# Pairs of experts' odd pieces in shared tiles: 73 tiles in place of 80 in a mixture-of-experts tower

## The reference

```python
probs = softmax(xt @ router_w.T + router_b)          # 16 experts
topk_p, topk_i = lax.top_k(probs, 2)                 # every row goes to two
gates = jnp.sum(onehot(topk_i) * topk_p[..., None], axis=1)
def expert_step(acc, (w1e, b1e, w2e, b2e, ge)):      # w1e 512x128, w2e 128x512
    h = gelu(xt @ w1e.T + b1e)
    y = h @ w2e.T + b2e
    return acc + y * ge[:, None]
```

## Time and profile before

| | us |
|---|---|
| median of 3 runs (671.29 to 671.98) | 671.81 |
| the profiled execution | 673.02 |
| its span, first to last instruction | 671.2 |
| TensorE busy | 615.3 (92%) |
| VectorE busy | 569.6 (85%) |
| ScalarE busy | 496.4 (74%) |
| GpSimd busy | 424.3 (63%) |
| mean granted clock of TensorE | 0.982 |

### The profile page before, as it was taken

One profiled execution on the slowest core, in us unless ns is written; L12 is line 12 of the kernel. 1 busy time (PEld: TensorE's weight loads), 2 busy tenths in 40 slices (PEclk: granted clock), 3 DMA queues, 4 the chain that ended last, 5 costly groups with the idle time before them and its releaser, 6 DMA issues.

```text
span 671.2 us, 24622 instructions
## 1 busy us (share of the span) xinstructions
PE 615.3 (92%) x7952; PEld 580.8 (87%) x7952; DVE 569.6 (85%) x1800; ACT 496.4 (74%) x1258; POOL 424.3 (63%) x446
## 2 busy tenths in 40 slices
PE   3899999999999999999998877999999999999970
PEld 3799999999999999999997866789988989888760
DVE  3888888888988888988899878997887887989896
ACT  3678888666776777676555457778888888999884
POOL 0244444488787786667666677777777666666571
PEclk9999999999999999999999979999999999999995
DMA  8988887778988888878876114445543435555665
GB/s 320 379 277 284 282 276 272 244 260 274 284 272 287 275 277 280 252 233 261 261 252 194 57 56 100 111 127 168 169 142 116 119 114 157 159 175 161 188 225 201
DMA packets 76063, 143.29 MB, mean 213 GB/s; under 512 B 14110, under 2 KB 59817, under 8 KB 68005
## 3 DMA queue, kind: packets, MB, share of 16 engines
q1 hardware_dynamic: 66080, 122.96, 58.6%
q0 software_dynamic: 9280, 17.21, 7.3%
q10 hardware_dynamic: 580, 1.55, 0.6%
HBM read 117.96 MB, written 25.66 MB: 214 GB/s over the span
## 4 chain that ended last, share of the span: by engine, by line
PE 54%; DVE 10%; issue 7%; DMA 5%; POOL 3%; ACT 1%; SPq 0%; POOLq 0%; DVEq 0%; ACTq 0%
PE pair L1298 19%; PE pair L1458 11%; PE pair L1476 10%; DMA patches<-sent 4%; PE pair L1344 3%; PE pair L1308 3%; PE pair L1432 2%; DVE patches L1114 2%; POOL sent L1250 1%; POOL back L1274 1%; PE pair L1313 1%; PE pair L1404 1%; PE pair L1373 1%; DMA field<-back 1%; PE pair L1323 1%
## 5 line engine op out<-in xcount | busy, mean ns | idle before, releaser
L1274 POOL DMA_INDIRECT back<-patches x160 | 156.7, 979 | 68.3 <-issue 53.9
L1250 POOL DMA_INDIRECT sent<-pay,slot_own x130 | 155.5, 1196 | 40.4 <-issue 38.2
L1298 PE MATMUL pair<-field,patches 128*128 128x128 f32 x1280 | 158.4, 280 | 9.0 <-DMA patches<-in_x 9.0
L1298 PEld LDWEIGHTS pair<-field,patches 128*128 128x128 f32 x1280 | 149.5, 194 | 9.0 <-issue 9.0
L685 ACT ACTIVATE pair<-pair,b1s 128x256 f32<-128x256 f32 x320 | 123.7, 448 | 28.4 <-PE pair L1458 26.5
L610 ACT ACTIVATE gate<-pair,lbias 128x128 f32<-128x128 f32 x260 | 74.3, 368 | 88.3 <-PE pair L1313 88.3
L1458 PE MATMUL pair<-patches,ex_hi 128*128 128x256 f16 x640 | 110.9, 275 | 5.4 <-DVE patches L1114 3.9
L1476 PE MATMUL pair<-ex_hi,patches 128*128 x1280 | 111.4, 219 | 2.9 <-DVE patches L1114 1.5
L1262 POOL TENSOR_TENSOR rstd<-veps,cst 128x2 f32<-128x2 f32 (+1 forms) x68 | 57.4, 845 | 84.5 <-DVE veps L813 84.1
L1298 PE MATMUL pair<-field 128*128 128x128 f16 x1664 | 103.4, 219 | 2.1 <-DVE field L856 2.1
L1298 PEld LDWEIGHTS pair<-field 128*128 128x128 f16 x1664 | 99.1, 98 | 3.1 <-issue 1.3
(11 more groups left out here) (152 smaller groups left out, 1232.6 us busy)
## 6 DMA issues: line engine op xcount, KB each, us to landing
patches<-in_x SPq DMA_DIRECT2D x62, 1152.0 KB
patches<-sent SPq DMA_DIRECT2D x80, 130.0 KB
field<-in_we SPq DMA_DIRECT2D x64, 128.0 KB
field<-back SPq DMA_DIRECT2D x10, 768.0 KB
patches<-in_b SPq DMA_DIRECT2D x80, 64.0 KB
field<-in_pos SPq DMA_DIRECT2D x65, 64.0 KB
out_tower<-h SPq DMA_DIRECT2D x10, 384.0 KB
patches<-in_x SPq DMA_DIRECT2D x128, 24.0 KB
```

Source lines behind the costliest of these rows:

```text
L1250: pool.indirect_dma_start(sent, bass.IndirectOffsetOnAxis(ap=slot_own[:, g % 4, choice, col:col + 1], axis=0), pay[:, t % NP, :], None, bo ...
L1274: pool.indirect_dma_start(back, bass.IndirectOffsetOnAxis(ap=dsti[j % NO][:, k:k + 1], axis=0), yo[j % NO][:, k, :], None, bounds_check=2 ...
L1298: last = pe.matmul(bank_of, l, w_, start=(c == 0), stop=(c == KC and k == 1))
```

## The change

The number of tiles goes from 80 to 73. Each expert's rows are now counted in pieces of 128: `HALVES_ALL` = 145 of them in the worst case, and TILES_B is half of that, rounded up. An expert's even number of pieces makes tiles of 256 rows as before. Its odd last piece, if there is one, goes into half of one of eight **dual** tiles (tiles 32, 35, ... 53), which hold the pieces of two experts.

- The late plan gets a fourth section of 16 entries (the odd pieces) and one for what lies between; it looks up 33 + 16 = 49 entries in place of 48. Its last three lines work from PSUM directly, in both plans, and the early plan's piece 8 and part of its piece 7 are gone, with the late plan computing what they did.
- A dual tile's rows come in two loads of 128 rows. Its second half's expert is copied by DMA from `ex_hi` and `ex_lo` to one of two fixed buffers, `at_hand`, which with a two-row bias buffer `b2_two` lies where `pay` was.
- TensorE does a dual tile's up matmuls as 24 of 128 columns, ScalarE its gelus as eight of 128x128, VectorE its destinations as two.
- Chunks: eight of 6 tokens, of which four begin in slots 60, 64, 68 and 72 and four are loaded in slots 74 to 77; then 17 tokens in four pieces (`LAST`, 5 + 4 + 4 + 4) after all scatters, into the memory of `ex_hi`.

```diff
-TILES_B = (2 * TOKENS - E) // ROWS + E
+HALVES_ALL = (2 * TOKENS - E) // P + E
+TILES_B = -(-HALVES_ALL // HALVES)
+DUALS = E // 2
+DUAL = tuple(range(EARLY, EARLY + 3 * DUALS, 3))
+PAIRS = TILES_B - EARLY - DUALS
+LOOKUPS = PAIRS + 2 * DUALS
-FIRST_SPAN, SECOND_SPAN = 32, 54
+FIRST_SPAN, SECOND_SPAN, GATED = 32, 48, 54
+CHUNKS = [(t, CHUNK) for t in range(0, SECOND_SPAN, CHUNK)]
+LAST = [(48, 5), (53, 4), (57, 4), (61, 4)]
-FIRST_IN = EARLY + E
-SECOND_IN = (2 * P * SECOND_SPAN - E) // ROWS + E
-BACK_AT = (52, 57, 62, 67, 71, 74)
+FIRST_IN = EARLY + E + DUALS
+SECOND_IN = (2 * P * SECOND_SPAN - E) // ROWS + E + DUALS
+BACK_AT = (60, 64, 68, 72)
...
-        LOADS = {**{at: m for m, at in enumerate(BACK_AT)}, 76: 6, 78: 7, 80: 8}
+        LOADS = {**{at: m for m, at in enumerate(BACK_AT)}, 74: 4, 75: 5, 76: 6, 77: 7}
... SyncE
+                    if j in DUAL:
+                        for half in range(HALVES):
+                            sp.reg_load(at_half, tabi[0:1, 1, k + half:k + half + 1])
+                            row = sp.snap(at_half, min_val=0, max_val=E * CAP)
+                            sp.dma_start(xt[j % 4][:, half, :], sent[bass.ds(row, P), :]).then_inc(xt_in[j % 4], 16)
+                j = n + 2
+                if j in DUAL:
+                    d = DUAL.index(j)
+                    if d >= 2:
+                        through(sp, down_ps, DUAL[d - 2])
+                        through(sp, y_done, DUAL[d - 2])
+                    k = column(j)
+                    sp.reg_load(at_other, tabi[0:1, 0, k + 1:k + 2])
+                    e = sp.snap(at_other, min_val=0, max_val=E - 1)
+                    for part_of, whole_of in enumerate((ex_hi, ex_lo)):
+                        sp.dma_start(at_hand[d % 2][:, part_of, :, :],
+                                     whole_of[:, bass.ds(e, 1), :, :].rearrange("p a m f -> p (a m) f")
+                                     ).then_inc(hand_in[d % 2], 16)
+                    sp.dma_start(b2_two[d % 2][:, 1, :],
+                                 b2[bass.ds(e, 1), :].rearrange("a h -> (a h)").partition_broadcast(P)
+                                 ).then_inc(b2_two_in[d % 2], 16)
...
             tiles_landed(sp, TILES_B)
-            for m in range(BETWEEN + AHEAD_OF_END, len(CHUNKS)):
-                load_back(m)
+            for k, (t, size) in enumerate(LAST):
+                sp.dma_start(last_rows[k], back.rearrange("(b r) h -> b r h", r=2 * T)[:, 2 * t:2 * (t + size), :]
+                             ).then_inc(last_in[k], 16)
             for m in range(BETWEEN, len(CHUNKS)):
                 store_out(m)
... ScalarE
+                width = ROWS // len(experts)
                 for i in range(2):
+                    for a, e in enumerate(experts):
+                        cols = slice(i * ROWS + a * width, i * ROWS + (a + 1) * width)
+                        last = act.activation(up[:, cols], up[:, cols], ACT.Gelu,
+                                              bias=b1s[:, bass.ds(e * FC + 2 * half + i, 1)], scale=1.0 / E_SCALE)
... VectorE, the late plan's first piece
+                        tiles_of(full, late, P - 1, cst[:, C_EBASE:C_TOK])
+                        by(late, dve.tensor_tensor(ceiled[:, :, :], ceiled[:, :, :],
+                                                   full.unsqueeze(1).to_broadcast([P, 2, E]), ALU.min))
+                        by(late, dve.tensor_tensor(odd_base, full, cst[:, C_EBASE:C_TOK], ALU.add))
+                        seen(late)
+                        by(late, dve.tensor_tensor(over[:, 0:E], count[:, :], odd_base, ALU.is_gt))
+                        by(late, dve.tensor_tensor(base[1], ceiled[:, 0, :], took[1], ALU.add))
+                        by(late, dve.tensor_tensor(lengths[:, 0:E], ceiled[:, 0, :], took[0], ALU.subtract))
+                        by(late, dve.tensor_tensor(lengths[:, 2 * E:3 * E], full, ceiled[:, 1, :], ALU.subtract))
+                        by(late, dve.tensor_tensor(base[2], ceiled[:, 1, :], cst[:, C_EBASE:C_TOK], ALU.add))
+                        seen(late)
... TensorE
+            def up_of_two(n, half, i, e):
+                d, c = DUAL.index(n), 2 * half + i
+                x_hi, x_lo = xTs[n % 2][:, 0:ROWS], xTs[n % 2][:, ROWS:2 * ROWS]
+                for a in range(HALVES):
+                    if a == 1 and half == 0 and i == 0:
+                        pe.wait_ge(hand_in[d % 2], (d // 2 + 1) * 32)
+                    rows = slice(a * P, (a + 1) * P)
+                    for k, (part_of, r) in enumerate(((0, x_hi), (0, x_lo), (1, x_hi))):
+                        if a == 0:
+                            w1 = (ex_hi, ex_lo)[part_of][:, bass.ds(e, 1), 0, c * P:(c + 1) * P].rearrange(
+                                "p a f -> p (a f)")
+                        else:
+                            w1 = at_hand[d % 2][:, part_of, 0, c * P:(c + 1) * P]
+                        last = pe.matmul(ps_up(n, half)[:, i * ROWS + a * P:i * ROWS + (a + 1) * P], w1, r[:, rows],
+                                         start=(k == 0), stop=(k == 2))
...
-                        for k, (h_, w_) in enumerate(((hhi, ex_hi), (hlo, ex_hi), (hhi, ex_lo))):
+                        for k, (h_, part_of) in enumerate(((hhi, 0), (hlo, 0), (hhi, 1))):
                             for a in range(HALVES):
+                                if a == 1 and j in DUAL:
+                                    w2 = at_hand[DUAL.index(j) % 2][:, part_of, 1, c * HID:(c + 1) * HID]
```

More of the change, by code:

```diff
@@ L305, in tower @@
         b2_in = [sem(f"b2_in{i}") for i in range(4)]
+        hand_in = [sem(f"hand_in{i}") for i in range(2)]
+        b2_two_in = [sem(f"b2_two_in{i}") for i in range(2)]
         in_ps, in_hi, in_done = sem("in_ps"), sem("in_hi"), sem("in_done")
@@ L315, in tower @@
         out_done = sem("out_done")
+        last_in = [sem(f"last_in{i}") for i in range(len(LAST))]
+        last_first, last_scaled, last_done = sem("last_first"), sem("last_scaled"), sem("last_done")
         N_FIRST, N_WEIGHTS, N_CONST = 2, 4, 3
@@ L323, in slots @@
         def slots(step, tile, steps_first=False):
-            for n in range(-5, AHEAD + TILES_B + 4):
+            for n in range(-5, AHEAD + max(TILES_B + 4, BACK_AT[-1] + 10)):
                 if n <= AHEAD or steps_first:
@@ L418, in tiles_landed @@
         def tiles_landed(eng, tiles):
-            for q in range(NO):
-                eng.wait_ge(y_out[q], 16 * HALVES * len(range(q, tiles, NO)))
+            for j in range(tiles - NO, tiles):
+                eng.wait_ge(y_out[j % NO], (j // NO + 1) * 16 * HALVES)
         def norms(n):
@@ L446, in _ @@
             at_row, at_expert, at_pad = (sp.alloc_register(name) for name in ("at_row", "at_expert", "at_pad"))
+            at_half, at_other = (sp.alloc_register(name) for name in ("at_half", "at_other"))
             def load_patches(t):
@@ L867, in step @@
                     dve.tensor_copy(padi[:, :], count[0:1, :]).then_inc(pad_rows, 1)
-                for span, g in enumerate((3, 6)):
+                for span, g in enumerate((3, 5)):
                     if n == ready(g) + 1:
@@ L1074, in plan_piece @@
                     seen(late)
+                    by(late, dve.tensor_scalar(expert, expert, odd_half, None, ALU.add))
+                    seen(late)
                 if k == 5:
@@ L1455, in step_b @@
                             c = 2 * half + i
+                            if n in DUAL:
+                                last = up_of_two(n, half, i, e)
+                                continue
                             for k, (w_, r) in enumerate(((ex_hi, x_hi), (ex_hi, x_lo), (ex_lo, x_hi))):
```

270 lines of the change are left out of this document (173 added, 97 removed).

## The result

The changed kernel took 665.64 us in the median of five runs (664.47 to 668.86), the kernel before 671.56 beside it on the same chip. The ratio is 0.9922, 95% interval 0.9900 to 0.9944: faster by 5.2 us by the ratio, 5.9 by the medians. The forecast was 659.5, a gain of 12.3. So the sign is right and the time lies just inside the range (up to 666.0), but less than half of the gain arrived.

A forecast was written before the change was run, and what follows sets the result against it. TensorE was taken to bound the main tile stretch at 2.952 us per tile. Terms -20.7 + 1.0 + 2.9 - 0.5 - 1.7 + 6.7 = -12.3 from 671.8 gave 659.5 us, range 655.5 to 666.

The forecast's parts named there:

- Seven tiles fewer: In the TensorE-bound stretch or the one behind it, seven tiles removed at 2.952 us each: -20.7 us.
- The early plan: Five operations of pieces 7 and 8 and one of piece 6 go, three move to slot 55: -0.5 us.
- The late plan: Operations added between tiles where VectorE has no idle time, so nothing hides them: +2.9 us, ends +1.5 and +3.9.
- The dual tiles on TensorE, ScalarE and VectorE: In eight dual tiles, narrow matmuls cost the same, and extra gelu and destination work fits in idle time: 0 us.
- The copies: SyncE's weight copies for dual tiles land just before TensorE wants them, with thin margin: +1.0 us, ends 0 to +6.
- The back phase: Loads of 768 KB from `back` delay gathered rows in three places instead of five: -1.7 us, ends -2.5 and 0.
- The tail: From the last bias addition (Y) to the end, Y + 26.3 against Y + 19.6: +6.7 us, ends +4.5 and +9.5.
- VectorE's path: In the tail, VectorE's remaining chunks, gates and 17 tokens, then 2.6 us to the end: Y + 25.4.
- the queue's path: In the tail, 8.5 MB to move, loads at 336 and stores at 390 GB/s, plus 2 us for scatters: Y + 26.
- Copies hold TensorE up: Rival: slow copies inside SBUF make TensorE wait before each dual tile's fourth up matmul; 679 us at 90 GB/s, chance 0.06.
- The long tail: Rival: the tail has more gathers than the queue can move, 8.5 MB at 285 GB/s: +11.2, 664.0 us, chance 0.15.
- the short one: Rival: VectorE's tail path of Y + 25.4 or less holds and copies cost nothing: tail +5, 656.1 us, chance 0.18.

The follow-up runs named there:

- the last experiment: The changed kernel with the late plan's pieces in every second slot, both dual-tile bias rows on ScalarE's queue and chunk 4 loaded earlier: 660.45 us, ratio 0.9820.
- the four traces: First trace of the changed kernel, the same kernel run again (665.82 us), and two later kernels with the same code up to the end of the duals.
- the kernel with the three edits together: The changed kernel with the second bias row on ScalarE's queue, GpSimd adding in chunks 6 and 7, and chunk 4 loaded earlier: 662.39 us, ratio 0.9874.

## Why the prediction was right or wrong

*Seven tiles fewer, -20.7: right.* Outside the changed places the period is unchanged, (501.50 - 457.27)/15 = 2.949 us.

*The early plan, -0.5: not contradicted.* Instance 0 came at 402.38 against 403.61; over all these traces at 402.0 to 403.6, 402.9 on average, so -0.7. The scatter is larger than that, so the traces don't tell -0.5 from nothing.

*The late plan, +2.9: right.* Instances 7 and 13 in VectorE's order of time, with the wait that ends the stretch:

```profile
427.88 1.21 DVE L1231 TENSOR_TENSOR patches<-pair,patches 128x1024 f16<-128x1024 f32 x1
...
450.12 0.42 DVE L1239 CAST patches<-pair 128x256 f16<-128x256 f32 x1 [0.97 <-PE pair L1585]
...
451.12 1.21 DVE L1231 TENSOR_TENSOR patches<-pair,patches 128x1024 f16<-128x1024 f32 x1
```

(451.12 - 427.88)/6 = 3.87 us per tile, where 3.9 was forecast against 3.41, and +3.0 for the stretch. "Nothing hides it" was right for the slots as they stood; the last experiment shows that the free slots beside them could.

*The dual tiles on TensorE, ScalarE and VectorE, nothing: right.* The stretch without copies runs at 53.12 for 18 tiles. The eight narrow gelus, forecast at 2.2 us, in ScalarE's order of time:

```profile
504.73 2.15 ACT L768 ACTIVATE pair<-pair,b1s 128x128 f32<-128x128 f32 x8 [0.49 <-PE pair L1569]
```

*The copies, +1.0: wrong, +5.0 in this trace and +4.2 on average, within the ends of 0 and +6.* This is the step that failed. The prediction asked whether the copies would land before TensorE wants them, 5.3 us after the first one's issue. In one of the four traces they always did, in another with one wait of 0.3; in the others TensorE waited for `ex_lo`, up to 0.72 and 0.99 us. In the changed kernel run again it landed 5.05 us after the first copy's issue (526.85 to 531.90), which is inside the 5.3, but the copies had left late, and TensorE wanted them 4.4 us after that issue.

The prediction wrote "SyncE is not late for others: its slot has 2.95 us and about 1.4 us more of issues; the bias of tile j-1 is wanted three slots on". The issues cost more: from 507.09, the end of the rows' issue, to 510.15, the end of the extra bias, 3.06 us, since the first copy's issue took 1.32 and the pause for the register load ahead of it 0.46. And the bias of tile j-1 isn't all that matters: behind it stand the rows of the next tile, in the same queue. They left at 511.73, 2.0 late against the pace of 2.95, and TensorE waited 0.52. Not counted either were the two loads of half a tile with a register load each, and that the three slots together hold ten issues. The prediction listed them in part, priced them as time for the copies, and didn't follow the queue on to the next tile.

What the experiments settle is that the copies make this whole cost. How it divides is rougher: about two thirds stay with a quarter of the bytes, and the long register loads of TensorE come and go with the bytes. Part of the cost shows as no wait at all: in 36 to 54 TensorE is busy 53.9 to 54.3 us in the four traces and 53.11 without copies, with the same matmuls, and why wasn't traced. What makes it differ by 2 us from trace to trace is open; single issues of 1.3 to 2 us, such as at 507.55, fall at other places in each, and without slack they would show, but that was only argued; the trace with a quarter of the bytes has four of 1.0 to 1.3 us in 36 to 54 as well.

Another small wait, about 0.2 us before the up matmuls, is put down to "issue". It falls on the matmul whose address depends on a register, and in the stretch 503 to 575 of this trace there are five of these, 1.1 us in all; in the kernel before there is none. Three of the five stand behind a wait for rows, the two others (548.60 and 567.60) behind a register load of 0.56 and 0.57 us. Where the kernel before waited for rows, from 577 us on, it has four of them as well, 0.9 us. In the kernel with one bias row on ScalarE there are five in 36 to 54 without any wait for a transfer.

*The back phase, -1.7: better, -3.3.* 54 to the last instance takes 54.10 = 18 x 2.951 + 1.0, where before it was 78.04 = 25 x 2.951 + 4.3. Of the loads that were thought to delay rows, at 0.8 each, one does so, by 0.3 us in TensorE's waits of this stretch.

*The tail, +6.7: right in kind, +8.2 in this trace.* VectorE in order of time, from the last bias addition to its last operation:

```profile
634.56 0.42 DVE L1246 SCALAR_TENSOR_TENSOR patches<-pair,patches 128x256 f32<-128x256 f32 x1 [0.33 <-PE pair L1635]
...
641.94 1.66 DVE L1312 SCALAR_TENSOR_TENSOR h<-field,gates,h 128x128 f32<-128x128 f32 x6 [0.78 <-DMA field<-back]
643.90 0.96 DVE L1323 TENSOR_TENSOR h<-h,field 128x768 f32<-128x768 f32 x1 [0.30 <-ACT field L755]
...
651.13 0.34 DVE L1298 TENSOR_REDUCE total<-lg 128x11 f32<-128x176 f32 x1 [0.74 <-ACT top L748]
...
659.10 0.69 DVE L1345 TENSOR_TENSOR h<-h,ex_hi 128x512 f32<-128x512 f32 x1
```

VectorE's path had been put at Y + 25.4 with 2.6 us after its last addition, so at Y + 22.8 for that addition. It ended at 659.79, Y + 25.2. The difference is its waits: 0.78 for chunk 4, and 1.6 for ScalarE (0.30 at 643.90 and at 649.43, 0.74 for the exponents, 0.27 at 653.64), which the sum had left out. Then 2.6 us to the end, as forecast. SyncE and the chain show the rest:

```profile
630.94 0.35 SPq L566 DMA_DIRECT2D out_tower<-h  x1
631.34 6.88 SPq L560 DMA_DIRECT2D field<-back  x3
```

```profile
638.73 8.71 DMA field<-back
```

Chunk 4's load stands behind the store of chunk 1, and chunk 7's, issued at 638.73, took 8.71 us, where the load that the kernel before issued at 658.79 took 4.63. The queue is full from 641 to 659 (share 1.01). Both paths of the forecast are there and near each other: relieving VectorE of two additions moved the end by nothing, and loading chunk 4 early moved VectorE's end by 1.1 us and the end by about half of that, or by nothing that one trace can tell. Which of the two is later in the last 3 us isn't settled; the last store's landing came 2.4 to 4.0 us after VectorE's end in these traces.

Beside the tail the prediction had set the Trainium skill (SBUF — State Buffer, "Summary: rules for kernel authors") with about 358 GB/s between HBM and SBUF. This tail moved 378 over 18 us and 400 in a stretch of 5 (645 to 650 us), loads and stores together by the view's count. The measurement is above the page, and it decides; the 378 lies between the 336 and the 390 that the queue's path took for loads and for stores. The prediction's remark that the fastest stretch of the trace before, 319 GB/s, stays below the page's figure was a misreading: that is the fastest of the tail, and the token phase of the same trace has this window.

```profile
16.00:33.00 17.00, 13.61 (x182) 12.76 (x183) 13.76 (x44) 9.99 (x28) 3.95 (x6) 1.00 1.04 380
```

That the queue would be no bound, as the page's rate had it, isn't borne out: it is full for 18 of the 27.8 us, with 27.84 x 322 = 8.96 MB to move, where 8.5 were counted.

*The rivals.* "Copies hold TensorE up" named the right cause and a part of the place: in the four traces no copy was near the 1.7 us late that would have cost the whole gain, and some waits are for the rows behind the copies. The long tail (+11.2) and the short one (+5) lie on both sides of +8.2. In sum, by the trace against the forecast: copies +4.0, tail +1.5, back phase -1.6, early plan -0.7, the rest +0.3, so 3.5 worse than -12.3. The other 2.9 between -8.8 and the medians' -5.9 lie in how each profiled execution stood to its median. The traces show two places that vary in the changed kernel, the dual stretch (2.1 us) and the tail; whether they explain all of it stays open.

## What to carry to other kernels

When a transfer is added to a queue-issuing engine, ask first for the next thing in its program order and how much slack that has, and sum the issues with their register loads over as many slots as the work repeats in; the new transfer's own time counts from when the queue comes to issue it. Its bytes can cost something apart from any wait for it, here in another engine's register loads. Work that an engine has to do between tiles costs less if it is cut so that free slots lie between the pieces. Before merging tensors to save a DMA, look at the addresses that other engines build from them.

## What the runs showed of the hardware

- An issue with a register-held address takes SyncE 0.33 to 0.54 us and about 0.45 more for its register load; single ones took 1.3 to 2.0 us (1.32 at 507.55, 1.47 at 536.97), at places that differ from trace to trace. I had counted 0.33.
- Two copies of 256 KB inside SBUF, one issued right behind the other: where TensorE waited for the second, it had landed 4.4 to 5.6 us after its issue (4.43, 4.84, 5.37 and 5.60 in four traces).
- TensorE's register load took 0.30 us, and in some slots 0.52 to 0.64 while such copies were on their way; with a quarter of their bytes it stayed at 0.30.
- After TensorE has waited for a DMA, a second gap of about 0.2 us follows in front of the next matmuls with register addresses (516.71 and 545.37 in the first trace); it also comes behind a long register load without such a wait.
- While GpSimd added 128x768 values (1.79 us from 647.50), six products of VectorE that began at 648.44, before that addition's end, took 2.31 us, against 1.66 alone; in the kernel with the three edits together they took 2.45.
